# A graph network's encoder on one core: turning the normalized x of pairs 2 to 5 off the matrix engine

## The chip, the core and the metric

The kernel runs on one core of one Trainium2 chip. The core has five engines with a queue each: TensorE (PE in the rows; its weight loads are PEld), VectorE (DVE), ScalarE (ACT), GpSimd (POOL) and SyncE (SP, which here only issues DMAs; SPq is its queue). They work side by side and meet at semaphores. The metric is the device time of one run in microseconds (us); less is better.

## The reference

1250 nodes with 1024 features, 40,000 edges of two types. A relational graph convolution comes first, then a residual network with an encoder, three graph layers and a decoder. The part that this case is about is the encoder:

```python
x = _layernorm(x + L0(x))                         # x1 in the kernel
# L1:
h = layernorm(x, ln_in_g, ln_in_b)                # (x - m) * rsqrt(v + eps) * g + b
h = relu(h @ W1 + b1)                             # 1024 -> 512
h = h @ W2 + b2                                   # 512 -> 256
for i in range(3):
    z = h + segment_sum(h[src], dst)              # then two small products, a norm, a residual
    ...
delta = relu(h @ Wd1 + bd1) @ Wd2 + bd2
return layernorm(x + delta, out_g, out_b)
```

## The kernel before, in words

The 1250 nodes are T = 10 tiles of P = 125 rows. The encoder takes them in five pairs, called chunks here: chunk c holds tiles 2c and 2c+1. Features must lie on the partitions for the product with W1, so each normalized tile is turned from [125 nodes x 1024] to eight blocks [128 features x 125].

For chunk c the work runs through four engines:

- **GpSimd** (`second_norm`, L368) writes the normalized tile, without gain and bias, into one of two buffers `xh`.
- **TensorE** (`turn_chunk`, L823) turns both tiles by 16 products with the identity into four PSUM banks (0 to 3). These are the MATMULs of L830.
- **ScalarE and VectorE** take them out of PSUM, times gain plus bias, into `hT`: ScalarE four of the 16 blocks (`weigh_first`, L523), VectorE twelve (`weigh_turned`, L1318, instructions of L1325).
- **TensorE** (`chunk_of_3`, L834) then multiplies W1 with `hT` in four groups f = 0 to 3 of eight products (L845; the trace counts two records for each fp32 product, so 64 a chunk; a transpose is one record), which alternate between banks 4 and 5; ScalarE takes each group out with a relu (`relus_of_3`, L532, instructions of L537). Group f + 2 waits for the relu of group f, since it uses its bank. Group 1 of chunk 0 also waits for `res_done` of the last tile (the residual sum of L1283), which frees bank 5. Then the product with W2 (L855, 16 records a chunk) waits for all four relus, and VectorE adds the bias into `h` (`first_h`, L1328).

TensorE's order in chunk c is: the four groups of W1, the transposes of chunk c + 1, the product with W2. Chunks 0 to 3 run in a loop, chunk 4 behind it; four of the five chunks so hold transposes, and those of chunk 0 stand ahead of the encoder.

The order is written by hand on every engine. Beside chunk 0, VectorE and ScalarE still finish the norms of the last tiles (`into_encoder`, L1350ff.): they pass small results to and fro, and ScalarE's relus of groups 0 and 1 stand between these steps in its queue. SyncE issues, in this order: W1 in four parts with the last tile of x, W2 (L316), `wa_s` (L329), three rows of 1024 spread over 125 partitions (`bd2_b`, `go_b`, `bo_b`, L332), two of 768 (`bb_b`, `ng_b`, L325), and after the encoder the next weights.

Of the kernel before, what the change touches and what calls it, by code (L numbers as in the profile page):

```python
# [25 lines left out]
P = 125  # L26
T = N // P
# [30 lines left out]
def graph_kernel(nc, x, src, dst, typ, ln_w, w_rel, w_root, conv_b, wo, g_in, b_in, w1, b1, w2, b2,  # L58
                 wa, ba, wb, bb, ng, nb, wd1, bd1, wd2, bd2, g_out, b_out, out):
    with ExitStack() as ctx:  # L60
# [60 lines left out]
        def x1(t):  # L121
# [14 lines left out]
        assert end <= adj1_end, (end, adj1_end)  # L136

# [11 lines left out]
        assert end4 <= root_base, (end4, root_base)  # L149
        (w5, junk), end = stack(y_base + size([P, T, HB], F32) + size([128, K2, HB], F32) + size([128, K1, 2 * P], F32), [  # L150
# [80 lines left out]
        half_done, out_half = sem("half_done"), sem("out_half")  # L231
        out_done = [sem(f"out_done{u}") for u in range(2)]
# [24 lines left out]

        def zeros(n):

            return zero[:, 0:1].rearrange("p (a b) -> p a b", a=1).broadcast_to([P, T, n])  # L260

        @block.sync
        def _(sp):
# [65 lines left out]
            sp.dma_start(wa_s[:], wa[0].rearrange("(k p) f -> p k f", p=128)).then_inc(wab_in, 16)  # L329
            sp.wait_ge(wo_mm, 1 + 2 * T)  # L330
# [4 lines left out]

            sp.wait_ge(h_mm, 1 + T)
# [20 lines left out]
        def _(pool):  # L357
# [11 lines left out]
            def second_norm(t):  # L369
                pool.wait_ge(ln2_shift, t + 1)  # L370
                if t >= 2:
                    pool.wait_ge(xhT_ps, 2 * t - 2)
                pool.tensor_scalar(xh[:, t % 2], x1(t), small2[:, 2, t:t + 1], small2[:, 3, t:t + 1],  # L373
                                   ALU.mult, ALU.add).then_inc(xh_ready, 1)
# [11 lines left out]
            for t in range(4):  # L386
                second_norm(t)
            pool.wait_ge(fin_in, 48)
            pool.tensor_tensor(bo_b[:], bo_b[:], bd2_b[:], ALU.subtract).then_inc(bo_less, 1)
            for c in range(T // 2):  # L390
                for t in (2 * c + 4, 2 * c + 5):
# [20 lines left out]
        def _(act):  # L412
# [118 lines left out]

            def relus_of_3(c, blocks):  # L532
                for f in blocks:
                    if f == 0:
                        act.wait_ge(h_mm, 1 + c * 2)
                    act.wait_ge(r1_mm, 1 + c * K1 + f + 1)
                    act.activation(r1T[:, f], pb[:, 4 + f % 2, 0:2 * P],  # L537
                                   ACT.Relu, bias=b1_c[:, f:f + 1]).then_inc(r1_done, 1)
# [24 lines left out]
            relus_of_3(0, range(2, K1))  # L563
# [5 lines left out]
            for c in range(1, T // 2):  # L569
                weigh_first(c)  # L570
                for t in (2 * c - 2, 2 * c - 1):
                    high_part(t, t + 1)
                relus_of_3(c, range(K1))
# [125 lines left out]
        def _(pe):  # L699
# [124 lines left out]
            def turn_chunk(c):  # L824
                for u in range(2):
                    pe.wait_ge(xh_ready, c * 2 + u + 1)
                    for q in range(2):
                        for i in range(4):
                            k = 4 * q + i
                            ins = pe.transpose(pb[:, 2 * u + q, i * P:(i + 1) * P],  # L830
                                               xh[:, u, k * 128:(k + 1) * 128], ident[0:P, 0:P])
                        ins.then_inc(xhT_ps, 1)

            def chunk_of_3(c, last):  # L834
                pe.wait_ge(hT_lo, 1 + c + 1)
                pe.wait_ge(hT_hi, 1 + c + 1)
                pe.wait_ge(r1_done, 1 + c * K1)
                for f in range(K1):
# [5 lines left out]
                    for k in range(KD):  # L844
                        ins = pe.matmul(pb[:, 4 + f % 2, 0:2 * P], w1_s[:, k, f * 128:(f + 1) * 128], hT[:, k],  # L845
                                        start=(k == 0), stop=(k == KD - 1))
                    ins.then_inc(r1_mm, 1)
                if not last:
                    turn_chunk(c + 1)
# [50 lines left out]
            with pe.Fori(0, T // 2 - 1) as c:  # L900
                chunk_of_3(c, False)
# [160 lines left out]
        def _(dve):  # L1062
# [265 lines left out]

            def first_h(c):
# [19 lines left out]
            def into_encoder():  # L1349

                dve.wait_ge(consts_in, 16 * 5)
                weigh_turned(0)
                first_shift(T - 2)
# [9 lines left out]
                weigh_turned(1)  # L1363
# [149 lines left out]
```

## Time and profile before

| | |
|---|---|
| median of 3 runs | 591.04 us (590.6 to 591.4) |
| the profiled execution | 590.85 us, of which the span of its core is 589.0 us |
| granted TensorE clock, mean | 0.994 of full speed; full in every stretch of the encoder |
| busy shares of the span | TensorE 97%, VectorE 65%, ScalarE 38%, GpSimd 15% |
| the encoder in the span | from 276.2 us (first product with W1) to 369.3 us (first product of the graph layer) |

In the rows, times are us from the start of the span, unless marked ns. A row of a timeline gives the start, the length and the engine of a run of like instructions, its line, what it writes and reads, and how many there were; brackets at its end give the idle time ahead of it and what ended it. Matmul records overlap, so the start of the next row tells more than the end of one.

### The profile page before, as it was taken

How to read it: one execution, taken by the hardware profiler on the slowest of the kernel's cores; microseconds unless marked ns; L12 is line 12 of the kernel's file. 1: busy time of each engine (PE TensorE's matmuls, PEld its weight loads, DVE VectorE, ACT ScalarE, POOL GpSimd, SP SyncE). 2: the span in 40 equal slices, each digit the busy share in tenths (PEclk: the TensorE clock that was granted, in tenths of full speed). 3: DMA queues.
4: the chain of work that ended last, by engine and by line, in shares of the span. 5: the costliest groups of instructions: out<-in, count | busy, mean ns of one | idle time of the engine just before them, and what ended most of it. 6: DMA issues, size and time to landing. Idle time of an engine off the chain costs nothing.

```text
span 589.0 us, 8351 instructions
## 1 busy us (share of the span) xinstructions
PE 570.4 (97%) x2582; PEld 394.8 (67%) x2582; DVE 385.1 (65%) x996; ACT 223.1 (38%) x455; POOL 88.5 (15%) x70
## 2 busy tenths in 40 slices
PE   7999999999999999999999999999999999999992
PEld 3565655555567677675888888877877867455540
DVE  8599999888857888889503330018748667755464
ACT  5444344432213546553412221012223134266555
POOL 3000000000000000003065513401202230132230
PEclk9999999999999999999999999999999999999997
DMA  8510011111031112128300000600100100021123
GB/s 268 144 36 7 28 36 35 35 35 35 0 83 45 35 42 66 35 79 215 139 37 0 0 0 1 221 3 2 38 0 0 36 1 0 2 70 53 53 70 105
DMA packets 20897, 30.74 MB, mean 52 GB/s; under 512 B 5441, under 2 KB 15155, under 8 KB 20864
## 3 DMA queue, kind: packets, MB, share of 16 engines
q1 hardware_dynamic: 20710, 30.07, 17.1%
q8 instruction: 17, 0.28, 0.2%
q10 hardware_dynamic: 154, 0.26, 0.1%
q14 instruction: 16, 0.13, 0.1%
HBM read 25.20 MB, written 5.12 MB: 51 GB/s over the span
## 4 chain that ended last, share of the span: by engine, by line
PE 88%; DVE 3%; issue 2%; DVEq 2%; ACT 1%; SPq 1%; DMA 1%; POOL 0%
PE banks L726 15%; PE banks L925 12%; PE banks L1011 12%; PE banks L845 12%; PE banks L815 5%; PE banks L874 5%; PE banks L712 5%; PE banks L876 4%; PE banks L947 4%; PE banks L937 4%; PE banks L855 3%; PE banks L1001 3%; PE banks L819 2%; DVEq L1164 1%; PE banks L830 1%
## 5 line engine op out<-in xcount | busy, mean ns | idle before, releaser
L726 PE MATMUL banks<-w_all,xnT 128*125 128x429 f32 x320 | 129.3, 527 | 0.4 <-DMA w_all<-in_L_gnn_W_rel 0.4
L726 PEld LDWEIGHTS banks<-w_all,xnT 128*125 128x125 f32 x320 | 54.0, 188 | 30.1 <-issue 28.4
L1182 DVE TENSOR_TENSOR adj<-adj,banks 125x220 f32 x160 | 60.8, 380 | 17.3 <-PE banks L712 17.0
L845 PE MATMUL banks<-hT,w_s 128*128 128x250 f32 x320 | 68.7, 375 | 0.1
L845 PEld LDWEIGHTS banks<-hT,w_s 128*128 128x128 f32 x320 | 60.2, 189 | 8.8 <-issue 1.9
L874 PE MATMUL banks<-y_hi,adj 125*125 125x288 f32 x200 | 55.2, 304 | 0.9 <-DVE small L1241 0.9
L712 PEld LDWEIGHTS banks<-oh_code,oh_low 125*128 125x128 bf16 x320 | 30.5, 97 | 35.8 <-issue 30.5
L876 PE MATMUL banks<-y_lo,adj 125*125 125x286 f32 x200 | 53.6, 295 | 0.0
L1154 DVE TENSOR_TENSOR oh_code<-iota_c,edge 125x880 bf16<-125x880 f16 x82 | 50.0, 610 | 0.0
L1325 DVE TENSOR_SCALAR hT<-banks,g_c,b_c 128x125 f32<-128x125 f32 x60 | 19.4, 401 | 45.1 <-PE banks L830 45.0
L925 PE MATMUL banks<-adj,h_hi 125*128 125x250 f32 (+1 forms) x180 | 48.2, 367 | 0.0
L373 POOL TENSOR_SCALAR xh<-x_first,small 125x1024 f32<-125x1024 f32 x6 | 7.4, 1238 | 260.5 <-DVE adj L1269 260.4
L712 PE MATMUL banks<-oh_code,oh_low 125*128 125x220 bf16 x320 | 44.7, 260 | 1.9 <-DVE oh_code L1154 0.9
L925 PE MATMUL banks<-adj,h_lo 125*128 125x250 f32 (+1 forms) x180 | 45.6, 353 | 0.0
L1011 PE MATMUL banks<-wd_s,dT 128*125 128x512 f32 x96 | 42.7, 592 | 0.0
L874 PEld LDWEIGHTS banks<-y_hi,adj 125*125 125x125 f32 x200 | 37.1, 186 | 7.7 <-issue 6.1
L434 ACT ACTIVATE xnT<-banks,lnw 128x125 f32<-128x125 f32 x80 | 22.6, 377 | 50.1 <-PE banks L720 50.1
L378 POOL TENSOR_TENSOR h_lo<-h,h_hi 125x256 fp32r<-125x256 f32 x30 | 21.8, 732 | 108.0 <-ACT h_hi L567 108.0
L876 PEld LDWEIGHTS banks<-y_lo,adj 125*125 125x125 f32 x200 | 37.3, 186 | 0.0
L815 PE MATMUL banks<-wo_s,yT 128*125 128x512 f32 x80 | 36.0, 592 | 0.0
L1150 DVE TENSOR_TENSOR oh_low<-iota_l,edge 125x512 bf16<-125x512 f16 x82 | 34.3, 419 | 0.2 <-issue 0.2
L925 PEld LDWEIGHTS banks<-adj,h_hi 125*128 125x128 f32 x180 | 29.8, 189 | 5.5 <-issue 1.4
(190 smaller groups left out, 875.0 us busy)
## 6 DMA issues: line engine op xcount, KB each, us to landing
xt<-in_x SPq DMA_DIRECT2D x15, 448.0 KB
out_x<-ot SPq DMA_DIRECT2D x9, 448.0 KB
w_s<-in_L_gnn_W SPq DMA_DIRECT2D x5, 512.0 KB, 5.9
xn<-in_x SPq DMA_DIRECT2D x5, 448.0 KB
wd_s<-in_L_gnn_Wd SPq DMA_DIRECT2D x1, 2048.0 KB, 13.1
w_all<-in_L_gnn_W_rel SPq DMA_DIRECT2D x6, 286.0 KB, 6.0
wo_s<-in_L_gnn_wo_weight SPq DMA_DIRECT2D x1, 1024.0 KB, 6.6
w_all<-in_L_gnn_W_root SPq DMA_DIRECT2D x3, 286.0 KB, 5.6
```

The costliest lines, as they stand in the source:

```text
L712: ins = pe.matmul(pb[:, b, q * R * C:(q + 1) * R * C], oh_low[:, b, q, :, j], oh_code[:, b, q, :, j], start=(j == 0), stop=(j == JH - 1))
L726: ins = pe.matmul(pb[0:P, 2 + 2 * v + n, 0:FH], xnT[:, u], w_all[:, u, n * FH:(n + 1) * FH], start=(u == 0), stop=(u == KD - 1))
L815: pe.matmul(pb[0:P, 5 + q], yT[:, i], wo_s[:, i, q * 512:(q + 1) * 512], start=(i == 0), stop=False)
L845: ins = pe.matmul(pb[:, 4 + f % 2, 0:2 * P], w1_s[:, k, f * 128:(f + 1) * 128], hT[:, k], start=(k == 0), stop=(k == KD - 1))
L874: pe.matmul(pb[0:P, b + r, 0:F + 2], mine, y_hi[:, s, r * (F + 2):(r + 1) * (F + 2)].bitcast(kind), start=(s == 0), stop=False)
L876: ins = pe.matmul(pb[0:P, b + r, w0:w0 + F], mine, y_lo[:, s, r * F:(r + 1) * F].bitcast(kind), start=False, stop=(s == T - 1))
L925: ins = pe.matmul(pb[:, 3 * f + c, 0:n], part[:, s, f * 128:(f + 1) * 128], adj[:, 0, s, c0:c0 + n], start=(s == 0 and part is h_hi), stop ...
L937: ins = pe.matmul(pb[:, 3 * f + c, 0:n], wa_s[:, k, f * 128:(f + 1) * 128], zT[:, k, c0:c0 + n], start=(k == 0), stop=(k == K2 - 1))
L1011: ins = pe.matmul(pb[0:P, 2 + 2 * u + q], (dT, dT_odd)[c % 2][:, k, u * P:(u + 1) * P], wd2_s[:, k, q * 512:(q + 1) * 512], start=(k == 0) ...
L1150: return dve.tensor_tensor(oh_low[:, b], both(iota_l, LOW), spread_out(edge[:, 0], g, LOW), ALU.is_equal)
L1154: return dve.tensor_tensor(oh_code[:, b], both(iota_c, R * C), spread_out(code, g, R * C), ALU.is_equal)
L1182: dve.tensor_tensor(cols, cols, window(b, q), ALU.add).then_inc(done, 1)
```

## The change

The transposes of chunks 1 to 4 leave TensorE. For these chunks:

- **VectorE** turns each `xh` tile in blocks of 32 by 32 (`turn_blocks`, one instruction for a tile, 128 partitions x 1024) into `xb`. Three rows of x are loaded once into partitions 125 to 127 of both `xh` buffers, so that they hold numbers. `xb` holds both tiles of a chunk.
- **SyncE** moves the blocks between the groups of 32 partitions (`move`): 16 DMAs a chunk from SBUF to SBUF, each 32 partitions x 2 tiles x 1 KB (64 KB, in 64 runs of 1 KB). They raise one semaphore by 256 in all.
- **ScalarE** applies gain and bias in place (`weigh_moved`, eight instructions 128 x 128 for a tile), one tile behind the relu of group 2 and one behind that of group 3 of the chunk before.
- **TensorE** multiplies W1 with `moved_to(c)`, which has 2 x 128 columns a block where `hT` has 250. The loops over chunks are written out. Chunk 0 keeps its transposes, its `hT` and its 250 columns.
- Odd chunks use the buffer `hT_m`, even ones `hT_z`, which shares its place with chunk 0's `hT`. The move of chunk 2 or later waits until the W1 product of the chunk before is through.
- GpSimd's norms of tiles 4 and 5 stand ahead of its wait for the spread rows, and later ones move up a chunk.

```diff
@@ SyncE
+            for u in range(2):
+                sp.dma_start(xh[P:128, u], x_t[0][0:128 - P]).then_inc(pad_in, 16)
...
             sp.dma_start(wa_s[:], wa[0].rearrange("(k p) f -> p k f", p=128)).then_inc(wab_in, 16)
+            def move(c):
+
+                sp.wait_ge(xb_turned, 2 * c)
+                if c >= 2:
+                    sp.wait_ge(r1_mm, 1 + (c - 1) * K1)
+                for g in range(4):
+                    for q in range(4):
+                        sp.dma_start(moved_to(c)[g * 32:(g + 1) * 32, :, q],
+                                     xb[q * 32:(q + 1) * 32, :, g]).then_inc(xb_moved, 16)
+
+            move(1)
             sp.wait_ge(wo_mm, 1 + 2 * T)
             for a, d in ((bd2_b, bd2), (go_b, g_out), (bo_b, b_out)):
...
+            for c in range(2, T // 2):
+                move(c)
@@ GpSimd
-                if t >= 2:
+                if 2 <= t < 4:
                     pool.wait_ge(xhT_ps, 2 * t - 2)
+                if t >= 4:
+                    pool.wait_ge(xb_turned, t - 3)
...
-            for t in range(4):
+            for t in range(6):
                 second_norm(t)
             pool.wait_ge(fin_in, 48)
@@ ScalarE
+            def weigh_moved(t):
+
+                c, u = t // 2, t % 2
+                act.wait_ge(xb_moved, 256 * c)
+                for k in range(KD):
+                    part = moved_to(c)[:, u, :, k * 32:(k + 1) * 32]
+                    ins = act.activation(part, part, ACT.Identity, scale=g_c[:, k:k + 1], bias=b_c[:, k:k + 1])
+                ins.then_inc(hT_set, 1)
...
-            relus_of_3(0, range(2, K1))
+            relus_of_3(0, [2])
+            weigh_moved(2)
+            relus_of_3(0, [3])
+            weigh_moved(3)
@@ TensorE, chunk_of_3
-                pe.wait_ge(hT_lo, 1 + c + 1)
-                pe.wait_ge(hT_hi, 1 + c + 1)
+                if c == 0:
+                    pe.wait_ge(hT_lo, 1 + 1)
+                    pe.wait_ge(hT_hi, 1 + 1)
+                else:
+                    pe.wait_ge(hT_set, 2 * c)
...
+                            ins = pe.matmul(pb[:, 4 + f % 2, 0:256].rearrange("p (u q n) -> p u q n", u=2, q=4), w,
+                                            moved_to(c)[:, :, :, k * 32:(k + 1) * 32], start=(k == 0), stop=(k == KD - 1))
                     ins.then_inc(r1_mm, 1)
-                if not last:
-                    turn_chunk(c + 1)
                 pe.wait_ge(r1_done, 1 + c * K1 + K1)
@@ VectorE
+            def turn_blocks(t):
+
+                u = t % 2
+                dve.wait_ge(xh_ready, t + 1)
+                if t < 4:
+                    dve.wait_ge(pad_in, 32)
+                else:
+                    dve.wait_ge(xb_moved, 256 * (t // 2 - 1))
+                dve.transpose(xb[:, u].rearrange("p g (k e) -> p k g e", e=32),
+                              xh[:, u].rearrange("p (k g e) -> p k g e", g=4, e=32)).then_inc(xb_turned, 1)
...
-            with dve.Fori(1, T // 2 - 1) as c:
-                weigh_turned(c + 1)
+            for c in range(1, T // 2):
+                if c + 2 < T // 2:
+                    turn_blocks(2 * c + 4)
+                    turn_blocks(2 * c + 5)
                 first_h(c)
-            first_h(T // 2 - 1)
```

Where it moves instructions is best seen in the order itself. VectorE at the entry to the encoder, before (L1325 is the taking out of chunk 0, L1295 and L1297 are norm constants, L1283 is the residual of the last tile, for which group 1 of chunk 0 waits):

```order
L1289 BN_AGGR mv<-st_99 125x2
L1325 TENSOR_SCALAR hT<-banks,g_c,b_c 128x125 x12
L1295 RECIPROCAL small_98<-small_98 125x1
L1297 SCALAR_TENSOR_TENSOR small_98<-mv,small_98 125x1
L1283 SCALAR_TENSOR_TENSOR xt<-xt,banks 125x1024
L1286 BN_STATS st_99<-xt 125x6
```

The same place now (L1393 is the instruction of `turn_blocks`, L1339 the residual):

```order
L1345 BN_AGGR mv<-st_99 125x2
L1381 TENSOR_SCALAR hT<-banks,g_c,b_c 128x125 x12
L1393 STREAM_TRANSPOSE xb<-xh 128x8x4x32 x2
L1351 RECIPROCAL small_98<-small_98 125x1
L1353 SCALAR_TENSOR_TENSOR small_98<-mv,small_98 125x1
L1339 SCALAR_TENSOR_TENSOR xt<-xt,banks 125x1024
L1342 BN_STATS st_99<-xt 125x6
```

Two transposes of 1024 columns stand ahead of the last residual and of all that follows it. The twelve instructions of `hT` for each of chunks 1 to 4 are gone, and two transposes a chunk stand in other places.

ScalarE from the relu of group 1 of chunk 0 on, before (L537 are relus, L520 the last norm's root, L528 the taking out, L567 the split of h):

```order
L537 ACTIVATE r1T<-banks,b_c 128x250
L520 ACTIVATE small_98<-mv,epsc 125x1
L537 ACTIVATE r1T<-banks,b_c 128x250 x2
L528 ACTIVATE hT<-banks,b_c,g_c 128x125 x4
L567 CAST h_hi<-h 125x256 x2
L537 ACTIVATE r1T<-banks,b_c 128x250 x4
```

And now (L580 are relus, L572 the instructions of `weigh_moved`):

```order
L580 ACTIVATE r1T<-banks,b_c 128x250
L554 ACTIVATE small_98<-mv,epsc 125x1
L580 ACTIVATE r1T<-banks,b_c 128x250
L572 ACTIVATE hT_m<-hT_m,b_c,g_c 128x4x32 x8
L580 ACTIVATE r1T<-banks,b_c 128x250
L572 ACTIVATE hT_m<-hT_m,b_c,g_c 128x4x32 x8
L580 ACTIVATE r1T<-banks,b_c 128x250
L613 CAST h_hi<-h 125x256 x2
L580 ACTIVATE r1T<-banks,b_c 128x250 x2
L572 ACTIVATE hT_z<-hT_z,b_c,g_c 128x4x32 x8
```

Eight instructions stand between the relu of group 2 and that of group 3, and eight behind it.

SyncE around the first move, now; before, the 16 DMAs of L356 were not there and nothing else differed:

```order
L335 DMA w_s<-in_L_gnn_W 128x4x256
L348 DMA wa_s<-in_L_gnn_layer_Wa 128x2x256
L356 DMA hT_m<-xb 32x2x256 x16
L362 DMA bd_b<-in_L_gnn_bd 125x1024
L362 DMA go_b<-in_L_gnn_out_g 125x1024
L362 DMA bo_b<-in_L_gnn_out_b 125x1024
L344 DMA bb_b<-in_L_gnn_layer_bb 125x768
L344 DMA ng_b<-in_L_gnn_layer_ng 125x768
L356 DMA hT_z<-xb 32x2x256 x16
```

The first move stands between `wa_s` and the spread rows, the second behind them.

## Rows read from the trace of the kernel before

**Rows 1.** The page: busy time, share of the span and instructions of each engine.

```profile
PE 570.4 (97%) x2582; PEld 394.8 (67%) x2582; DVE 385.1 (65%) x996; ACT 223.1 (38%) x455; POOL 88.5 (15%) x70
```

**Rows 2.** Chain of waits, 300 to 440 us: start, length, what.

```profile
314.09 13.72 PE banks L845 x64
327.81 1.71 PE banks L830 x16
329.52 3.46 PE banks L855 x16
...
365.42 0.48 ACT r1T L537
...
365.94 3.72 PE banks L855 x16
```

**Rows 3.** Timeline of TensorE, chunk 0 and the last chunk.

```profile
276.17 13.76 PE L845 MATMUL banks<-hT,w_s 128*128 128x250 f32 x64
289.77 1.87 PE L830 MATMUL banks<-ident,xh 125*128 125x125 f32 x16
291.48 3.62 PE L855 MATMUL banks<-w_s,r1T 128*125 128x256 f32 x16
295.16 13.76 PE L845 MATMUL banks<-hT,w_s 128*128 128x250 f32 x64
...
351.70 13.69 PE L845 MATMUL banks<-hT,w_s 128*128 128x250 f32 x64
365.94 3.72 PE L855 MATMUL banks<-w_s,r1T 128*125 128x256 f32 x16 [0.56 <-ACT r1T L537]
```

**Rows 4.** Timeline of VectorE at the entry to the encoder.

```profile
271.94 3.88 DVE L1325 TENSOR_SCALAR hT<-banks,g_c,b_c 128x125 f32<-128x125 f32 x12
...
275.93 0.16 DVE L1297 SCALAR_TENSOR_TENSOR small<-mv,small 125x1 f32<-125x1 f32 x1
276.21 1.22 DVE L1283 SCALAR_TENSOR_TENSOR xt<-xt,banks 125x1024 f32<-125x1024 f32 x1
...
282.59 0.16 DVE L1295 RECIPROCAL small<-small 125x1 f32<-125x1 f32 x1 [1.24 <-ACT small L509]
```

**Rows 5.** Timeline of ScalarE beside chunk 0.

```profile
270.16 1.49 ACT L528 ACTIVATE hT<-banks,b_c,g_c 128x125 f32<-128x125 f32 x4
...
281.93 0.45 ACT L537 ACTIVATE r1T<-banks,b_c 128x250 f32<-128x250 f32 x1
...
285.75 0.45 ACT L537 ACTIVATE r1T<-banks,b_c 128x250 f32<-128x250 f32 x1
...
287.65 0.45 ACT L537 ACTIVATE r1T<-banks,b_c 128x250 f32<-128x250 f32 x1
```

**Rows 6.** Groups of ScalarE by shape, from 200 us on: SBUF to SBUF.

```profile
L567 ACT CAST h_hi<-h 125x256 fp32r<-125x256 f32 x30 | 12.2, 406 | 41.5 <-DVE h L1425 24.3 <-DVE h L1332 17.2
L514 ACT ACTIVATE x_rest<-x_rest,small 125x1024 f32<-125x1024 f32 x3 | 3.7, 1239 | 0.0
```

**Rows 7.** Stretches: busy time of each engine, clock, DMA share, GB/s.

```profile
276.00:282.00 6.00, 5.96 (x30) 5.27 (x29) 4.62 (x10) 1.41 (x3) 0.00 (x0) 1.00 0.94 265
...
286.00:290.00 4.00, 4.00 (x22) 3.51 (x21) 1.70 (x5) 0.88 (x4) 0.00 (x0) 1.00 0.32 129
...
298.00:302.00 4.00, 4.00 (x20) 3.59 (x19) 0.00 (x0) 0.47 (x1) 4.00 (x4) 1.00 0.08 26
```

**Rows 8.** Timeline of SyncE's queue: start and length of an issue.

```profile
279.01 0.71 SPq L325 DMA_DIRECT2D bb_b<-in_L_gnn_layer_bb  x1
...
369.69 0.39 SPq L319 DMA_DIRECT2D wb_s<-in_L_gnn_layer_Wb  x1
```

**Rows 9.** DMA issues of the whole span: count, KB each, median us to landing.

```profile
bd_b<-in_L_gnn_bd SPq DMA_DIRECT2D x1, 500.0 KB
...
bb_b<-in_L_gnn_layer_bb SPq DMA_DIRECT2D x1, 375.0 KB
...
ba_c<-in_L_gnn_layer_ba SPq DMA_DIRECT2D x3, 1.0 KB, 2.8
```

More of the change, by code:

```diff
@@ L136, in graph_kernel @@
         assert end <= adj1_end, (end, adj1_end)
+        (xb,), end = stack(z_base, [("xb", [128, 2, 4, 32 * KD], F32)])
+        assert end <= adj1_end
         adj_x = at(top[0], "adj_x", [P, R, T, ND], F32)
@@ L149, in graph_kernel @@
         assert end4 <= root_base, (end4, root_base)
+        z_zt = end4 - sum(size(a, F32) for a in ([P, 5, HB], [P, 2, 6], [P, 8], [P, 2, 2], [P, 2, 4], [P, 2, 4], [P, 2, 4]))
+        (hT,), end = stack(z_zt, [("hT", [128, KD, 2 * P], F32)])
+        (hT_z,), end = stack(z_zt, [("hT_z", [128, 2, 4, 32 * KD], F32)])
+        assert end <= root_base
         (w5, junk), end = stack(y_base + size([P, T, HB], F32) + size([128, K2, HB], F32) + size([128, K1, 2 * P], F32), [
@@ L231, in graph_kernel, with moved_to @@
         half_done, out_half = sem("half_done"), sem("out_half")
+        pad_in, xb_turned, xb_moved, hT_set = sem("pad_in"), sem("xb_turned"), sem("xb_moved"), sem("hT_set")
+        def moved_to(c):
+            return hT_m if c % 2 else hT_z
         out_done = [sem(f"out_done{u}") for u in range(2)]
@@ L256, in load_w, with r1_of @@
                               w_rel[r, part].rearrange("(k p) f -> p k f", p=128)).then_inc(w_in[q], 16)
+        def r1_of(c, f):
+            n = 128 if c else P
+            return pb[:, 4 + f % 2, 0:2 * n].rearrange("p (u n) -> p u n", u=2)[:, :, 0:P]
         def zeros(n):
@@ L390, in _ @@
             for c in range(T // 2):
-                for t in (2 * c + 4, 2 * c + 5):
+                for t in (2 * c + 6, 2 * c + 7):
                     if t < T:
@@ L536, in relus_of_3 @@
                     act.wait_ge(r1_mm, 1 + c * K1 + f + 1)
-                    act.activation(r1T[:, f], pb[:, 4 + f % 2, 0:2 * P],
+                    act.activation(r1T[:, f].rearrange("p (u n) -> p u n", u=2), r1_of(c, f),
                                    ACT.Relu, bias=b1_c[:, f:f + 1]).then_inc(r1_done, 1)
@@ L569, in _ @@
             for c in range(1, T // 2):
-                weigh_first(c)
+                relus_of_3(c, [0])
                 for t in (2 * c - 2, 2 * c - 1):
                     high_part(t, t + 1)
-                relus_of_3(c, range(K1))
+                relus_of_3(c, [1, 2])
+                if c + 1 < T // 2:
+                    weigh_moved(2 * c + 2)
+                relus_of_3(c, [3])
+                if c + 1 < T // 2:
+                    weigh_moved(2 * c + 3)
             for t in (T - 2, T - 1):
@@ L844, in chunk_of_3 @@
                     for k in range(KD):
-                        ins = pe.matmul(pb[:, 4 + f % 2, 0:2 * P], w1_s[:, k, f * 128:(f + 1) * 128], hT[:, k],
-                                        start=(k == 0), stop=(k == KD - 1))
+                        w = w1_s[:, k, f * 128:(f + 1) * 128]
+                        if c == 0:
+                            ins = pe.matmul(pb[:, 4 + f % 2, 0:2 * P], w, hT[:, k], start=(k == 0), stop=(k == KD - 1))
+                        else:
+                            ins = pe.matmul(pb[:, 4 + f % 2, 0:256].rearrange("p (u q n) -> p u q n", u=2, q=4), w,
+                                            moved_to(c)[:, :, :, k * 32:(k + 1) * 32], start=(k == 0), stop=(k == KD - 1))
                     ins.then_inc(r1_mm, 1)
-                if not last:
-                    turn_chunk(c + 1)
                 pe.wait_ge(r1_done, 1 + c * K1 + K1)
@@ L898, in _ @@
             project(T - 1)
-            with pe.Fori(0, T // 2 - 1) as c:
+            for c in range(T // 2 - 1):
                 chunk_of_3(c, False)
@@ L1352, in into_encoder @@
                 weigh_turned(0)
+                turn_blocks(2)
+                turn_blocks(3)
                 first_shift(T - 2)
@@ L1362, in into_encoder @@
                 dve.wait_ge(adj_self, T)
-                weigh_turned(1)
+                turn_blocks(4)
+                turn_blocks(5)
                 first_h(0)
```

11 lines of the change are left out of this document (6 added, 5 removed).

## The prediction

> **What bounds the kernel now.** The page's busy shares come first: TensorE is busy for 97% of the span [rows 1]. The chain of waits over the encoder says the same of this stage: it stays on TensorE through the chunks, and the transposes of L830 are a piece of it, 1.71 us in each of four chunks [rows 2]. So work taken off TensorE there can shorten the time. The next view is TensorE's timeline, which gives the period of a chunk: from 295.16 to 351.70 three chunks pass, 18.85 us each [rows 3]. The last chunk has no transposes, and it shows what they cover: behind group 3 TensorE is idle for 0.56 us until the relu is through [rows 2, 3]. The timelines of VectorE and ScalarE beside chunk 0 come last, for there the change puts new work into queues that TensorE waits for. The reader should see how near they run: group f of chunk 0 is due at 276.17 plus 3.40 f (279.57, 282.97, 286.37; a quarter of 13.60, the distance from 276.17 to 289.77 [rows 3]). The relus that groups 2 and 3 wait for end at 282.38 and 286.20 [rows 5], and the residual for group 1 at 277.43 [rows 4]. The spare time is 0.6, 0.2 and 2.1 us.
>
> **What chunks 1 to 3 gain.** Gone are 1.71 us of transposes. Exposed instead is the wait for the last relu. The last chunk is the model: from its first product with W1 to its first with W2 are 365.94 - 351.70 = 14.24 us, and W2 takes 3.46 [rows 2, 3]. That is 17.70 us. The columns go from 250 to 256. By columns the 13.72 us would grow by 0.33; by the pace of L855, whose records have 256 columns (3.46 / 16 = 0.216 us against 13.72 / 64 = 0.214 [rows 2]), by 0.12. I take 0.2. The period is 17.9 us, 0.95 less than before, and three of them give 2.85 us. The last chunk only pays the 0.2. The loops that are written out I cost at nothing, since TensorE shows no idle time at a chunk's seam [rows 3].
>
> The Trainium skill, in "VectorE: DVE Perf Modes", section "The three transpose paths", lists 390 ns on TensorE for a block of 128 by 128 and 311 ns on VectorE, bf16. By that VectorE would be the cheaper place. This trace has 107 ns for one of TensorE's 16 transposes, 1.71 / 16 [rows 2], and no transpose by VectorE at all, so it bears out no such advantage; the sum goes by the nearest rows, next.
>
> **What chunk 0 pays on VectorE.** Two transposes of 1024 columns stand ahead of the last residual. The nearest row is another VectorE instruction of 1024 columns, 1.22 us [rows 4]; with the gap to the next, 1.25 each, 2.5 in all. The bounds: 512 columns' worth each, 0.6 (1.2 in all), were it to go at twice that pace; and 0.316 us for each of the eight blocks of 128, the pace of the twelve instructions of L1325 (3.88 us [rows 4]), 2.5 each, 5.0 in all. The value is the nearest row's. VectorE was free at 276.09 and the residual began at 276.21 [rows 4], so 0.1 is absorbed and everything behind shifts by 2.4. It does shift: from there VectorE and ScalarE hand each other the norms of the last tiles (a wait of 1.24 us of VectorE for ScalarE stands among them [rows 4]), and the relus of groups 0 and 1 stand in ScalarE's queue between these steps [rows 5]. Then:
> - group 1 waits for the residual, which ends at 279.8: due 279.57, stall 0.3;
> - group 2 waits for the relu that now ends at 284.8: due 283.3, stall 1.5; it ends at 288.2;
> - group 3 waits for the relu that now ends at 288.6: stall 0.4; it ends at 292.0.
>
> **What chunk 0 pays on ScalarE.** The relu of group 2 starts at 287.65 + 2.4 = 290.05 and ends at 290.5. Then come eight instructions 128 x 128, SBUF to SBUF. The four of L528 take 1.49 us; if one is as long as a relu, 0.45, they follow each other at (1.49 - 0.45) / 3 = 0.35 us [rows 5]. The two SBUF shapes, 406 ns for 256 columns and 1239 for 1024, give 1.085 ns a column and 0.27 us for 128 [rows 6]. So 2.1 to 2.8; I take 2.75, near the row of the same operation. The relu of group 3 runs from 293.2 to 293.7, and W2 begins at 293.75 instead of 291.48, 1.7 us after group 3 has ended. The next chunk begins 3.5 later, at 297.25: 2.1 us later than the 295.16 of before. The transposes of chunk 1, 1.71 us, are already taken off in that. The second eight end by 296.5, ahead of chunk 1.
>
> **The moves.** The last VectorE transpose ends at 278.25. An issue takes 0.39 us on a quiet queue and 0.71 on a busy one [rows 8], with 0.04 between. W2 and wa_s are still under way until about 282 [rows 7]. At 0.42, 16 issues end at 285.0; at 0.75, at 290.2. Landing comes 2.8 us after the issue, by the smallest transfer [rows 9], from about 287.4 to 292.6. Needed is 290.5: with the faster pace nothing is paid. No row shows a copy from SBUF to SBUF.
>
> Behind the first move stand the spread rows, 3 x 500 + 2 x 375 KB = 2.30 MB [rows 9]. They run at 129 GB/s with a DMA share of 0.32, 5 of 16 engines [rows 7]: 17.9 us, and by the windows they ended at about 298.8 (26 GB/s over 298 to 302). Now they begin at about 285.5 and end at 303.4. The second move is issued from 293.2 on (VectorE turns tiles 4 and 5 after its last norm, at 290.6 to 293.1), behind them in the same queue. On the five engines its 64 runs of 1 KB each take 62 ns at the rate of 265 GB/s over 16 engines [rows 7], 4.0 us, so it lands at about 307.4 plus a tail of 1, 308.4. ScalarE can take it at 308.1 (297.25, three groups of 3.45, a relu), and group 3 ends at 311.05, so 2.75 us of work is hidden if it begins by 308.3. Between 0 (all of it early) and 3 us (busy issue pace, below) I take 0.3. The moves of chunks 3 and 4 have some 5 us to spare even though the last waits for chunk 2's product, and VectorE's waits for them stand ahead only of the bias of h, which is wanted a chunk later.
>
> The Trainium skill, "DMA: Bandwidth & Descriptors", section "Why a DMA increments its semaphore by 16 and not by 1", says that a DMA is split over the largest number up to 16 that divides its outer sizes: 125 partitions use 5 engines, 32 use 16. The trace agrees for the spread rows (0.32 of 16). The Trainium skill has further, on the same page under "Queues, rings and completion order", that each engine takes its ring in order, by which the second move can't pass them; no run shown here tests that.
>
> **The sum.** +2.1 (start of chunk 1), -2.85 (periods of chunks 1 to 3), +0.2 (last chunk), +0.3 (second move): -0.25 us. What follows the encoder starts from the same state as before. The profiled execution took 590.85 us, which gives 590.6; it lies 0.19 below the median of the runs, which gives 590.8, my forecast.
>
> **The rivals.**
> - *The full saving comes through* (faster). ScalarE's eight take 2.1 instead of 2.75, the second move is in time, VectorE's transpose goes a little faster (1.1), W1's pace is 0.12 dearer instead of 0.2. The terms: 2.1 - 0.65 - 0.3 = 1.15; -3.1; 0.12; 0. Sum -1.85, 589.2. For it: each term has a row on that side. Against: all must fall so. Chance 0.28, over 589.0 to 589.8.
> - *The second move decides* (slower). One place, ScalarE's wait ahead of the relu of group 3 of chunk 1; it costs from a landing after 308.3 on, one for one, and TensorE stands still. At the busy pace of 0.75 us the first move ends its issue at 290.2 and lands at 292.6, 2.1 late in chunk 0; chunk 1 starts at 299.35 and its limit is 310.4. The spread rows end at 290.6 + 17.9 = 308.5, the move lands at 313.5, 3.1 late. Sum -0.55 + 2.1 + 3.1 = +4.65, 595.7 at the full price; with only half of that delay some 593. For it: 0.71 us for an issue beside full traffic, and an unseen kind of copy. Against: the queue is quiet from 282 on. Chance 0.18.
> - *VectorE's transpose is twice as dear*, 2.5 us each (slower): 2.4 more through chunk 0, while the second move then is in time: -0.55 + 2.5 = +1.95, 593.0. The Trainium skill's 311 ns a block ("VectorE: DVE Perf Modes", "The three transpose paths"), eight of them, would be 2.5 us, an estimate from that page; it is for one block an instruction and need not hold for eight in one. For this rival speaks the pace of L1325, against it the 1.22 us of one instruction of 1024 columns [rows 4]. Chance 0.12.
> - *The change doesn't do what it says*: the order shows that the transposes are gone. No chance is left for it.
>
> The forecast has 0.42. About 0.2%, 1.2 us, is what a measurement of this kernel can tell from no change. Faster: most of the first rival and a little of the forecast's spread, 0.28. Slower: the second and third, 0.29. The same: 0.43. The range from 588.9 to 593.3 leaves out the full price of the second rival.
>
> **What would show it.** The line that L830 has become should have 16 records (chunk 0's) and take 1.7 us; TensorE idle times of about 0.3, 1.5, 0.4 and 1.7 us in chunk 0, the last three ended by ScalarE, and 0.56 us in each later chunk; a VectorE transpose of 1.2 us; ScalarE's instructions of `weigh_moved` 0.35 apart; periods of 17.9 us. The forecast is wrong if the issues of a move take over 0.6 us each, if ScalarE waits for a DMA ahead of `weigh_moved(2)` or `(4)`, if W1 with 256 columns in runs of 32 takes over 14.1 us, or if the stages behind the encoder move.

## The result, and the profile after

The changed kernel takes 603.53 us (median of 5 runs, 602.96 to 604.4), the kernel before 591.04 us (five runs too). The ratio is 1.0215, with a 95% interval of 1.0204 to 1.0226: slower by 12.5 us. The forecast was 590.8 us, with 588.9 to 593.3 as its range. It was wrong in size and in kind. The second rival, that the second move decides, is what happened, at more than twice the price that I gave it, and not by its path: it had the first move land late, at 292.6, and that one landed at 290.7. The profiled execution took 604.39 us, with a span of 602.1 us against 589.0.

The timeline of TensorE after the change, which answers to [rows 3], shows where the 13.1 us between the two spans lie (L901 and L903 are W1, with 250 and 256 columns; L911 is W2):

```profile
276.11 7.11 PE L901 MATMUL banks<-hT,w_s 128*128 128x250 f32 x32
284.51 3.65 PE L901 MATMUL banks<-hT,w_s 128*128 128x250 f32 x16 [1.29 <-ACT r1T L580]
288.34 3.65 PE L901 MATMUL banks<-hT,w_s 128*128 128x250 f32 x16 [0.18 <-ACT r1T L580]
294.35 3.72 PE L911 MATMUL banks<-w_s,r1T 128*125 128x256 f32 x16 [2.36 <-ACT r1T L580]
297.91 13.98 PE L903 MATMUL banks<-hT_m,w_s 128*128 128x256 f32 x64
322.31 6.16 PE L911 MATMUL banks<-w_s,r1T 128*125 128x256 f32 x16 [10.42 <-ACT r1T L580]
328.31 13.98 PE L903 MATMUL banks<-hT_z,w_s 128*128 128x256 f32 x64
342.84 3.72 PE L911 MATMUL banks<-w_s,r1T 128*125 128x256 f32 x16 [0.56 <-ACT r1T L580]
346.40 13.98 PE L903 MATMUL banks<-hT_m,w_s 128*128 128x256 f32 x64
...
364.49 13.98 PE L903 MATMUL banks<-hT_z,w_s 128*128 128x256 f32 x64
...
382.39 0.92 PE L981 MATMUL banks<-adj,h_hi 125*128 125x250 f32 x3
```

From the start of chunk 0 to that of chunk 1 are 21.80 us instead of 18.99 [rows 3]: +2.8. Chunk 1 takes 30.40 instead of 18.85: +11.55. Chunks 2 and 3 take 18.09 each: -0.76 each. The last, up to the first product of the graph layer, takes 17.90 instead of 17.6: +0.3. Together that is 13.1, the difference of the spans. The gain that the change is made for is there, in the two chunks that nothing disturbs. One chunk loses nearly eight times what these two gain.

TensorE's idle time of 10.42 us in chunk 1 is put down to ScalarE's relu. The relu was not slow; the chain of waits of the changed kernel tells what stood ahead of it:

```profile
294.26 5.26 SPq L356
...
310.56 0.60 SPq L356
...
311.20 7.49 DMA hT_z<-xb
...
318.72 3.18 ACT hT_z L572 x8
321.90 0.36 ACT r1T L580
322.31 6.16 PE banks L911 x16
```

The first issue of the second move holds SyncE's queue for 5.26 us, the last one begins at 310.56, and its data lands 7.49 us after 311.20. Only then do ScalarE's eight instructions run, and only behind them the relu. SyncE's queue, which answers to [rows 8]:

```profile
278.16 11.17 SPq L356 DMA_DIRECT2D hT_m<-xb  x16
289.38 0.49 SPq L362 DMA_DIRECT2D bd_b<-in_L_gnn_bd  x1
...
291.10 3.06 SPq L344 DMA_DIRECT2D ng_b<-in_L_gnn_layer_ng  x1
294.26 17.54 SPq L356 DMA_DIRECT2D hT_z<-xb  x16
321.18 10.74 SPq L356 DMA_DIRECT2D hT_m<-xb  x16
342.36 10.18 SPq L356 DMA_DIRECT2D hT_z<-xb  x16
```

Sixteen issues of a move take 10.2 us with nothing in their way and 17.5 behind the spread rows. The stretches of the changed kernel, which answer to [rows 7] (columns as there), show the traffic and the clock:

```profile
298.00:300.00 2.00, 2.00 (x11) 1.77 (x10) 0.43 (x2) 0.00 (x0) 0.00 (x0) 1.00 0.32 131
...
312.00:316.00 4.00, 0.00 (x0) 0.00 (x0) 0.00 (x0) 0.00 (x0) 4.00 (x3) 1.00 0.38 91
316.00:320.00 4.00, 0.00 (x0) 0.00 (x0) 1.22 (x2) 1.28 (x4) 0.95 (x1) 0.63 0.03 9
320.00:324.00 4.00, 1.69 (x4) 1.41 (x5) 1.16 (x2) 4.00 (x11) 2.37 (x2) 0.50 0.19 47
324.00:328.00 4.00, 4.00 (x12) 3.16 (x12) 0.42 (x1) 1.33 (x4) 0.00 (x0) 0.59 0.41 101
```

At 298 the spread rows run at a share of 0.32 and 131 GB/s, as before, but they were issued 13 us later (from 289.38 instead of 276.28). And the granted clock, full all through the encoder before, falls while TensorE stands still for 10.42 us (0.63 on average from 316 to 320) and is 0.50 from 320 to 324, 1.2 GHz instead of 2.4. W2 of chunk 1 takes 6.16 us instead of 3.72, so 2.4 us of the loss are the clock.

### The profile page after: what moved, and what is told of

Its sections match the earlier page's. It is cut to its first block, busy times and chain, and to the rows that moved or that the text cites. A ratio compares the mean times of both kernels' runs of the same rounds, so it can differ in the third digit from the quotient of the medians.

```text
span 602.1 us, 8227 instructions
## 1 busy us (share of the span) xinstructions
PE 568.8 (94%) x2518; PEld 390.0 (65%) x2518; DVE 379.2 (63%) x956; ACT 240.8 (40%) x503; POOL 88.5 (15%) x70
## 4 chain that ended last, share of the span: by engine, by line
PE 78%; SPq 6%; DVE 5%; DMA 3%; ACT 3%; issue 2%; DVEq 2%
PE banks L777 14%; PE banks L981 12%; PE banks L1067 11%; PE banks L903 6%; PE banks L866 5%; PE banks L763 4%; SPq L356 4%; PE banks L1003 4%; PE banks L993 4%; PE banks L930 4%; PE banks L932 4%; PE banks L911 3%; PE banks L1057 3%; PE banks L870 2%; DVEq L1220 1%
## 5 line engine op out<-in xcount | busy, mean ns | idle before, releaser
L1399 DVE TENSOR_TENSOR h<-banks,b_b 125x256 f32<-125x256 f32 x10 | 4.2, 425 | 56.3 <-PE banks L911 56.3
L911 PE MATMUL banks<-w_s,r1T 128*125 128x256 f32 x80 | 21.0, 422 | 14.5 <-ACT r1T L580 14.5
L981 PEld LDWEIGHTS banks<-adj,h_lo 125*128 125x128 f32 x180 | 30.1, 189 | 4.6
```

The costliest lines, as they stand in the source:

```text
L911: ins = pe.matmul(pb[0:P, 6 + u, 0:HB], r1T[:, k, u * P:(u + 1) * P], w2_s[:, k], start=(k == 0), stop=(k == K1 - 1))
L981: ins = pe.matmul(pb[:, 3 * f + c, 0:n], part[:, s, f * 128:(f + 1) * 128], adj[:, 0, s, c0:c0 + n], start=(s == 0 and part is h_hi), stop ...
```

## The experiments

All ratios are to the kernel before, timed beside them.

**What holds the second move.** In `e1_parts` the spread rows are loaded in two DMAs each:

```diff
-                sp.dma_start(a[:], spread(d)).then_inc(fin_in, 16)
+                for rows in row_parts:                     # 112 and 13 partitions
+                    sp.dma_start(a[rows], spread(d)[rows]).then_inc(fin_in, 16)
```

(and so for `bb_b`, `ng_b`, `nb_b`, with the waits for them doubled).

> The changed kernel, with each of the five spread rows loaded in two DMAs, 112 and 13 partitions, instead of one of 125. Theory A (the spread rows, on 5 of 16 DMA engines, hold the second move back in the same rings): on 16 engines their 2.3 MB are through in about 8 us, the second move lands by 307, and TensorE's idle time of 10.42 us ahead of W2 of chunk 1 shrinks to about 0.56, with no fall of the granted clock. Time 603.5 - 9.9 - 2.4 (W2 at full clock) = about 591.2 us. Theory B (a move is slow by itself: 0.64 us an issue and a slow copy from SBUF to SBUF): the idle time stays above 8 us and the time within 1.5 us of 603.5.

Measured: 593.33 us (592.48 to 593.95), ratio 1.0038 [1.0025, 1.0051]; 10.2 us less than the changed kernel, 2.1 more than theory A had. TensorE's timeline of `e1_parts`, and SyncE's queue:

```profile
294.65 3.72 PE L914 MATMUL banks<-w_s,r1T 128*125 128x256 f32 x16 [2.40 <-ACT r1T L583]
298.21 13.98 PE L906 MATMUL banks<-hT_m,w_s 128*128 128x256 f32 x64
312.74 3.72 PE L914 MATMUL banks<-w_s,r1T 128*125 128x256 f32 x16 [0.56 <-ACT r1T L583]
```

```profile
294.87 10.20 SPq L358 DMA_DIRECT2D hT_z<-xb  x16
```

The idle time of 10.42 us is 0.56, W2 has its full clock, and the second move's issues take 10.20 us, not 17.54. Nothing of the moves themselves was changed. So the spread rows, which kept 5 of the 16 engines busy, held it. In `e1_parts` the DMA share is 0.90 from 292 to 296, at 267 GB/s, and the last of the three rows of 1024 is in after 9.8 us (289.7 to 299.5) instead of 16.9.

The run tells something else: with the stall gone, the change is still slower than the kernel before, by 1.2 us of span. Chunk 0 is 2.9 us longer, three periods of 18.09 give back 2.3, the last chunk costs 0.3; the rest of the 1.2 stands outside these. The median lies 0.85 above the profiled execution, which was the fastest run and had the highest mean clock (0.995; the slowest, 593.95, had 0.991). The kernel before with the same edit, `b2_parts`, is the control:

> The kernel before, with only the five spread rows in 112 and 13 partitions. Nothing waits for them in the kernel before, so no change: within 0.3 us of it. If it is faster, e1_parts and all built on it owe that part to something else than the moves.

Measured: 591.06 us (590.67 to 591.76), ratio 1.0002 [0.9993, 1.0011]: no change.

**Rings or engines.** `e2_act_rows` takes the five rows from SyncE and has ScalarE issue them, ahead of its `second_sd(T - 3)`:

```diff
+            act.wait_ge(rel0_added, T)
+            act.wait_ge(wo_mm, 1 + 2 * T)
+            for a, d in ((bd2_b, bd2), (go_b, g_out), (bo_b, b_out)):
+                act.dma_start(a[:], spread(d)).then_inc(fin_in, 16)
...
```

> The changed kernel, with the five spread rows issued by ScalarE's queue at about 276 us, where ScalarE idles, instead of by SyncE behind the first move. They still use 5 engines, but rings of their own, and start 13 us earlier. Theory A: the second move is in time (idle ahead of W2 of chunk 1 about 0.56 us); the first move now shares the five engines with the rows and lands 2 to 4 us later than at 290.7, which TensorE waits for in chunk 0. Time 593 to 595 us. Theory B: both moves as slow as before, 603 us. If ScalarE's five issues take more than 5 us in all, chunk 0 gets longer by what is over.

Measured: 606.02 us (605.04 to 606.27), ratio 1.0246 [1.0231, 1.0262]. Both of my theories missed. The second move is in time (0.56 us in chunk 1), but it was issued from 305.36 on, when the rows were through, so this does not speak for theory A. And the first move is far later than I expected. ScalarE and TensorE of `e2_act_rows`:

```profile
302.86 3.19 ACT L567 ACTIVATE hT_m<-hT_m,b_c,g_c 128x128 f32<-128x128 f32 x8 [12.58 <-DMA hT_m<-xb]
```

```profile
306.46 5.43 PE L913 MATMUL banks<-w_s,r1T 128*125 128x256 f32 x16 [14.37 <-ACT r1T L575]
```

It lands at 302.8 instead of 290.7, with the rows under way at 120 to 133 GB/s from 292 until about 304, at a share of 0.31 to 0.34, five of 16 engines. A queue of its own for the rows does not free the move. Nor does it help to put the rows behind the second move, `e3_rows_later` (GpSimd's wait for them moves too, behind its low parts of chunk 0):

```diff
+            move(2)
             for a, d in ((bd2_b, bd2), (go_b, g_out), (bo_b, b_out)):
...
-            for c in range(2, T // 2):
+            for c in range(3, T // 2):
                 move(c)
```

> The changed kernel, with the five spread rows issued behind the second move instead of ahead of it, and GpSimd's wait for them behind its low parts of chunk 0. Theory A: the second move lands at about 306 and chunk 1 has no stall but 0.56 us; the third move now stands behind the rows and lands late, at 327 to 333, so that chunk 2 stalls by up to 6 us. Time 592 to 599 us. Theory B: chunk 1 still stalls for 8 us or more, 602 us or more.

Measured: 598.03 us (595.75 to 599.39), ratio 1.0108 [1.0085, 1.0131]. Chunk 1 has its 0.56 us, and the stall stands in chunk 2, 3.35 us, as theory A says. ScalarE and TensorE of `e3_rows_later`:

```profile
331.64 3.19 ACT L573 ACTIVATE hT_m<-hT_m,b_c,g_c 128x128 f32<-128x128 f32 x8 [2.70 <-DMA hT_m<-xb]
```

```profile
335.23 5.41 PE L912 MATMUL banks<-w_s,r1T 128*125 128x256 f32 x16 [3.35 <-ACT r1T L581]
```

The third move's issues were not held up here (10.60 us for 16), and yet it landed 7.2 us after the last of them. So a move behind the rows is late also where its issuer is free. Part of the scatter is probably the clock: in the profiled run it fell with the 2.46 us stall in chunk 0 and again in chunk 2 (W2 took 5.21 and 5.41 us instead of 3.72). In the changed kernel's and in `e1_parts`' profiled run a stall of about the same length left the clock at full. So a stall of 2.4 us in chunk 0 costs W2 1.5 us in some runs and nothing in others.

**What an issue costs.** `e5_split` cuts each DMA of a move in two, on top of `e1_parts`:

```diff
-                        sp.dma_start(moved_to(c)[g * 32:(g + 1) * 32, :, q],
-                                     xb[q * 32:(q + 1) * 32, :, g]).then_inc(xb_moved, 16)
+                        for u in range(2):
+                            sp.dma_start(moved_to(c)[g * 32:(g + 1) * 32, u, q],
+                                         xb[q * 32:(q + 1) * 32, u, g]).then_inc(xb_moved, 16)
```

> Built on e1_parts. Each DMA of a move is cut in two, one a tile: 32 DMAs of 32 KB (32 runs of 1 KB) in place of 16 of 64 KB. If the 0.60 us of an issue are a fixed price of a DMA from SBUF to SBUF, a move's issues take 20 us and chunks stall: 600 us or more. If they go by the runs, an issue takes about 0.3 us and nothing changes: 593. A copy whose pace goes by bytes on the engines would leave the issues at 0.4 and the landing where it is.

Measured in a single run: 624.7 us. TensorE stalls in each of chunks 0 to 3, by 12.48, 5.45, 5.38 and 4.12 us. The queue of `e5_split`:

```profile
278.26 21.45 SPq L359 DMA_DIRECT2D hT_m<-xb  x32
```

An issue of 32 runs takes 0.59 us in the median, one of 64 runs 0.60. So for these two sizes it is a fixed price of a DMA from SBUF to SBUF, where a load from HBM took 0.39 [rows 8].

**What chunk 0 pays.** `b1_turns` is the kernel before, with two transposes by VectorE and nothing else:

```diff
                 weigh_turned(0)
+                for t in (2, 3):
+                    dve.wait_ge(xh_ready, t + 1)
+                    dve.transpose(xb[0:96, t % 2]..., xh[0:96, t % 2]...)
                 first_shift(T - 2)
```

> The kernel before, with nothing changed but two transposes by VectorE (tiles 2 and 3, 96 partitions x 1024, result unused) ahead of the last residual. Theory A: they take 1.2 us each and shift the chain of the last norms by 2.1 us; TensorE stalls for 1.3 us ahead of group 2 and 0.2 us ahead of group 3 of chunk 0, as in the changed kernel: +1.5 us, 592.5. Rival: they are hidden, and the stalls come from something else of the change: 591.0.

Measured: 592.94 us (592.74 to 593.45), ratio 1.0028 [1.0016, 1.004], so +1.6 us, as theory A says. Its TensorE timeline has the same two stalls as the changed kernel (its chunk 0 as a whole is 2.0 us longer: 21.00 instead of 18.99):

```profile
284.72 3.65 PE L847 MATMUL banks<-hT,w_s 128*128 128x250 f32 x16 [1.29 <-ACT r1T L539]
288.55 3.65 PE L847 MATMUL banks<-hT,w_s 128*128 128x250 f32 x16 [0.18 <-ACT r1T L539]
```

The rest of chunk 0's loss is ScalarE's. `s1_share`, on top of `e1_parts`, gives one tile of each pair to VectorE and puts ScalarE's behind the relu of group 3:

```diff
-            relus_of_3(0, [2])
-            weigh_moved(2)
-            relus_of_3(0, [3])
+            relus_of_3(0, [2, 3])
             weigh_moved(3)
@@ VectorE
+                for k in range(KD):
+                    part = moved_to(c)[:, 0, :, k * 32:(k + 1) * 32]
+                    ins = dve.tensor_scalar(part, part, g_c[:, k:k + 1], b_c[:, k:k + 1], ALU.mult, ALU.add)
```

> Built on e1_parts. VectorE applies gain and bias to the first tile of each moved pair, ScalarE only to the second, behind the relu of group 3. Theory: in e1_parts ScalarE's eight instructions (3.19 us) ahead of the relu of group 3 of chunk 0, released by the first move at 290.7, cost 2.40 - 0.56 = 1.84 us of TensorE's time, and the same stall lowers the granted clock in part of the runs. Both go: idle of 0.56 us ahead of W2 of chunk 0, all later periods 18.09 as they were, 593.3 - 1.8 - 0.6 = about 591 us. Rival: the first move lands too late for chunk 1 in any case, and the stall only moves to the head of chunk 1: above 592.5.

Measured: 589.93 us (589.67 to 590.28), ratio 0.9983 [0.9974, 0.9992]. W2 of chunk 0 waits for 0.56 us. This is the first of the series that beats the kernel before, by 1.0 us, about 1 us better than its theory had.

**Covering the last relu.** `s2_ahead` has TensorE do group 0 of the next chunk ahead of W2, from chunk 1 on (`groups_of_3` and `second_of_3` are the two halves of `chunk_of_3`):

```diff
+            for c in range(1, T // 2):
+                groups_of_3(c, range(1, K1))
+                if c + 1 < T // 2:
+                    groups_of_3(c + 1, [0])
+                second_of_3(c)
```

> Built on s1_share. From chunk 1 on, TensorE does group 0 of the next chunk ahead of W2, so that this covers the last relu; VectorE weighs ten of the 16 blocks of a pair and ScalarE six, ahead of the relu of group 3. Theory: the 0.56 us exposed in chunks 1 to 3 go, 1.7 us in all: about 589.5 us, periods of 17.5 us. Rival: the gain is used up by waits for the blocks (moves land too late for group 0, which starts 3.5 us earlier): 591 or more.

Measured: 590.03 us (589.44 to 592.4), ratio 0.9988 [0.9978, 0.9998]. The time lies between what theory and rival had, no better than `s1_share`; the mechanism is the rival's. Periods of later chunks are 17.26 us (355.82 less 338.56), but group 0 of chunk 2 waits for its blocks, 2.39 us, and the clock is lower in some runs (a mean of 0.990 and 0.991 in the three slowest, at least 0.993 in the others).

`s3_shift` also has ScalarE take 12 of the 16 blocks of chunk 0 out of PSUM and VectorE only four, so that VectorE's transposes begin at 273.3 instead of 275.9:

```diff
+                act.wait_ge(xhT_ps, c * 4 + 4)
+                for k in range(KD):
+                    ins = act.activation(hT[:, k, P:2 * P], pb[:, 2 + k // 4, ...], ACT.Identity, ...)
@@ VectorE, weigh_turned
-                for u, q in ((0, 1), (1, 0), (1, 1)):
+                for u, q in ((0, 1),):
```

> Built on s2_ahead. In chunk 0 ScalarE, idle there until 282, takes 12 of the 16 transposed blocks out of PSUM and VectorE four, so that VectorE's two transposes begin 2.5 us earlier. Theory: the stalls of TensorE ahead of groups 2 and 3 of chunk 0 (1.29 and 0.18 us) come from those transposes shifting the chain of the last norms by 2.1 us; they shrink to 0.3 or less, the first move begins 2 us earlier, and the time falls by 1.2 us against s2_ahead, to about 588.3. Rival: the stalls stay, since ScalarE's part of the chain is what is late: no change.

Measured: 589.42 us (587.47 to 592.82), ratio 0.9984 [0.9968, 1.0]. The theory had 588.3. Chunk 0's stall of 1.29 us is gone, as it says, but the one in chunk 2 grew to 2.92 and the times scatter over 5 us, the slow ones again at the lower mean clock (0.989 to 0.992). To see the shift by itself, `s5_share_shift` puts it on `s1_share`, without group 0 ahead:

> s1_share with ScalarE's larger part in chunk 0 from s3_shift, and TensorE's order left as it was. Theory: s1_share has no late move, so the one stall that is left (1.29 us ahead of group 2 of chunk 0) goes: 589.9 - 1.2 = 588.7 us, and all runs near each other, since nothing lowers the clock. Rival: the scatter of s3_shift (587.5 to 592.8) comes from the shift itself: it scatters here too.

Measured: 588.72 us (588.28 to 588.84), ratio 0.996 [0.9947, 0.9974]: as expected, and steady.

**The late blocks of chunk 2.** `s4_issue` is `s3_shift` with four of a move's 16 DMAs issued by ScalarE's queue, and nine blocks of 16 for VectorE instead of ten:

```diff
+            def move_rest(c):
+                act.wait_ge(xb_turned, 2 * c)
+                act.wait_ge(r1_mm, 1 + (c - 1) * K1)
+                for q in range(4):
+                    act.dma_start(moved_to(c)[96:128, :, q], xb[q * 32:(q + 1) * 32, :, 3]).then_inc(xb_moved, 16)
```

> s3_shift with four of the 16 DMAs of moves 2 to 4 issued by ScalarE's queue at the head of a chunk, where ScalarE idles, and 9 blocks by VectorE, 7 by ScalarE. Theory: an issue costs 0.64 us of the issuing queue, so the second move lands 2.5 us earlier, and the wait of 2.9 us ahead of group 0 of chunk 2, with the fall of the clock behind it, goes: 587 us, without runs above 589. Rival: DMAs of two queues share the engines and land no earlier: as s3_shift.

Measured: 588.94 us (588.32 to 589.47), ratio 0.9963 [0.9949, 0.9976]. The theory had 587. The blocks land at 306.0, 1.6 us earlier and not 2.5, and the wait is still 1.99 us. VectorE of `s4_issue`, chunk 1's blocks and chunk 2's, and two instructions of the latter by themselves:

```profile
290.81 2.40 DVE L1422 TENSOR_SCALAR hT_m<-hT_m,g_c,b_c 128x128 f32<-128x128 f32 x9 [1.27 <-DMA hT_m<-xb]
...
305.96 5.26 DVE L1422 TENSOR_SCALAR hT_z<-hT_z,g_c,b_c 128x128 f32<-128x128 f32 x9 [9.82 <-DMA hT_z<-xb]
```

```profile
305.96 1.15 DVE L1422 TENSOR_SCALAR hT_z<-hT_z,g_c,b_c 128x128 f32<-128x128 f32 x1 [9.82 <-DMA hT_z<-xb]
307.03 2.39 DVE L1422 TENSOR_SCALAR hT_z<-hT_z,g_c,b_c 128x128 f32<-128x128 f32 x1
```

and GpSimd's:

```profile
304.67 4.67 POOL L420 TENSOR_TENSOR x_first<-x_first,bd_b 125x1024 f32<-125x1024 f32 x2
```

The first of nine instructions takes 1.15 us and the second 2.39 instead of 0.34. They end, within 0.1 us, when GpSimd's first and second one end (its two take 2.36 each, from 304.67 and 306.98 on), and with the other seven at their usual pace that is the whole 5.26. `s6_apart` keeps the two engines apart:

```diff
+                if c + 2 < T // 2:
+                    pool.wait_ge(hT_vec, c + 2)
                 for t in (2 * c, 2 * c + 1):
                     with_bd2(t)
```

> s4_issue with one wait more: GpSimd adds the row bd2 to a pair of tiles only after VectorE has applied gain and bias to its blocks of the next pair but one. Theory: in s4_issue VectorE's nine instructions took 5.26 us ahead of chunk 2 and 2.40 us ahead of chunk 1, because one of them waited for a GpSimd instruction that was running; kept apart they take 2.4 us, group 0 of chunk 2 starts without the idle time of 1.99 us, and the time falls by 2 us to about 587.0. Rival: the slowness comes from the spread rows' or the moves' DMA traffic, and stays: 588.9.

Measured: 586.53 us (586.42 to 588.52), ratio 0.9933 [0.992, 0.9947], 4.5 us less than the kernel before. VectorE and TensorE of `s6_apart`:

```profile
305.76 2.40 DVE L1424 TENSOR_SCALAR hT_z<-hT_z,g_c,b_c 128x128 f32<-128x128 f32 x9 [10.09 <-DMA hT_z<-xb]
```

```profile
295.03 13.98 PE L919 MATMUL banks<-hT_m,w_s 128*128 128x256 f32 x64
308.84 3.68 PE L919 MATMUL banks<-hT_z,w_s 128*128 128x256 f32 x16
312.36 3.62 PE L929 MATMUL banks<-w_s,r1T 128*125 128x256 f32 x16
315.81 10.52 PE L919 MATMUL banks<-hT_z,w_s 128*128 128x256 f32 x48
```

The blocks land when they did in `s4_issue` (305.8), so DMA traffic, the rival, was not what slowed VectorE. TensorE waits for nothing between 295.03 and the last chunk's relu.

## Why the prediction was wrong, point by point

- **Periods of chunks 2 and 3: right in kind, a gain of 0.76 us a chunk where I had 0.95.** 18.09 us, forecast 17.9. The wait for the last relu is 0.56 us as in the last chunk of before. W1 with 256 columns in runs of 32 costs 0.29 us a chunk (342.84 - 328.31 = 14.53, before 14.24), where I took 0.2 of 0.12 to 0.33. The other 0.1 is W2: I took its 3.46 from the chain, but from its first product to the next chunk's first are 3.57 in the kernel before (332.93 - 329.36) and 3.56 now.
- **VectorE's price in chunk 0: right.** A transpose takes 1.22 us, as the nearest row said. The stalls ahead of groups 2 and 3 are 1.29 and 0.18, forecast 1.5 and 0.4, the 0.3 ahead of group 1 did not come, and `b1_turns` shows them to be the transposes' alone. The rival that VectorE's transpose is twice as dear is out.
- **ScalarE's price in chunk 0: right in kind, too small.** Idle 2.36 us ahead of W2, forecast 1.7. The eight instructions are 0.39 us apart (3.19 us for eight, one of them 0.48), not 0.35, and the first move landed at 290.7, 0.6 later than they could begin. Chunk 1 began at 297.91, forecast 297.25.
- **The step that failed: "The moves", the landing of the second one.** I had it at 308.4 against a limit of 308.3, and gave 0.3 us. It landed at 318.7, 10.3 later. Three terms were mis-sized. The issue: 0.60 us with 0.04 between, not the 0.42 that I took from a load on a quiet queue, so that the spread rows began at 289.4 instead of 285.5 (3.9 us). The passage of the rows: I reckoned 17.9 us from their bytes and a rate of 129 GB/s. The third one landed at 306.3, and the last two, 750 KB, need 6.0 at that rate (an estimate), so they were through at about 312.3, after 22.9 us (5.0 more). And the move behind them landed 6.4 us later, where I had 4 and a tail of 1 (1.4 more). `e1_parts` shows that the rows on five engines make the whole of the stall.
- **What the rows of before had said.** In the kernel before the five rows were issued from 276.28 on, and GpSimd could use the third at 293.90, 17.6 us later:

```profile
276.28 0.38 SPq L332 DMA_DIRECT2D bd_b<-in_L_gnn_bd  x1
```

```profile
293.90 2.36 POOL L389 TENSOR_TENSOR bo_b<-bo_b,bd_b 125x1024 f32<-125x1024 f32 x1 [20.89 <-DMA bo_b<-in_L_gnn_out_b]
```

By my own reading of [rows 7] they ended at about 298.8. That is 22.5 us from the first issue, and not the 17.9 of the rate, though part of that time was shared with W2 and `wa_s`. From 289.4 it gives 311.9, and a landing near 317.
- **What I left out: the clock.** I priced a late landing one for one. Behind 10.42 us of standing still TensorE runs at 1.2 GHz for W2, 2.4 us more. The two together are the +11.55 us of chunk 1 with the gain of that chunk taken off: 9.86 + 2.44 - 0.76 = 11.54.
- **The sum without the failed step.** From chunk 0 +2.8, three periods -2.3, the last chunk +0.3: about +0.8 us, where I had -0.55. So even a second move in time would have made the kernel no faster, and `e1_parts` bears that out.
- **The signs.** Of those that I named, one came: ScalarE waits for a DMA ahead of `weigh_moved(2)` (0.57 us) and of `weigh_moved(4)` (9.78 us). An issue of a move, at 0.60 us, stands at the bound that I gave.
- **The chances.** The second rival had 0.18 and 595.7 as its full price. An estimate that ends 0.1 us past its limit, for a transfer of a kind that the trace does not show, is as likely late as not. The rival deserved more than 0.18, and the range should have reached at least to its full price; even that lies 7.8 us below what was measured.
- **Slips in the sums**, which change nothing: by its own terms the second rival's first move lands at 292.3, not 292.6 (278.25 + 15 x 0.75 + 2.8), and the first rival adds up to -1.83.

The Trainium skill, "DMA: Bandwidth & Descriptors", section "Queues, rings and completion order", says that an engine goes round its queues packet by packet. `e2_act_rows` agrees in so far as the rows, in a queue of their own, still share engines with the move, which landed 12 us later. In what turns the engines served the two queues, no run here shows.

What stays open: why the first three spread rows take longer than their bytes at 129 GB/s, 11.9 us for 1.54 MB. It was 16.9 us in the changed kernel, 16.2 in `e3_rows_later` (303.9 to 320.1) and 17.6 in the kernel before. From 290 to 298 the changed kernel has a share of 0.32 to 0.35, as at full rate, but only 102 to 104 GB/s. Open too is what SyncE's slowed issues, 17.5 us instead of 10.2, added to the last 1.4 us; `e1_parts` removes both at once and does not part them. A variant with fewer DMAs a move, each over 128 partitions, wasn't tried. Nor do the runs tell why a stall of 2.4 us lowers the clock in some runs only.

## What to carry to other kernels

Work taken off the busiest engine is paid for in the queues that take it over: ask of each new wait what else uses the same DMA engines, and when they are through, by the landing in a trace and not by bytes and a rate. In this case a load spread over 125 partitions kept five of the 16 engines busy for long and made a move behind it late; the same load as 112 and 13 partitions let it through (593.3 us instead of 603.5). And a step that is timed to land within a microsecond of its limit should be moved, or given an even chance of being late.

## What the runs showed of the hardware that I had not expected

- A DMA from SBUF to SBUF held the issuing queue for 0.60 us with 64 runs of 1 KB and for 0.59 with 32 (medians of `e1_parts` and `e5_split`), with 0.04 between two; the five spread rows, loads from HBM behind the first move, took 0.34 to 0.49 where nothing held them up.
- A VectorE instruction from SBUF to SBUF with one tensor input (128 x 128, float32) waited for a running GpSimd instruction to end: 2.39 us instead of 0.34 (`s4_issue`). Kept apart, none took over 0.35 (`s6_apart`). The Trainium skill, "SBUF — State Buffer", section "Who interferes with whom", tells of a port pair that VectorE and GpSimd share and that one holds for a whole instruction; these rows agree with it. Not every instruction waits: two of VectorE's transposes took 2.36 us together from 308.07 on in `s6_apart`, as ever, beside GpSimd's instructions of the same kind (308.23 to 312.91). In the kernel before VectorE took these blocks from PSUM, 0.40 us each in all 60 instructions.
- TensorE's clock fell from 2.4 to 1.2 GHz in each of the three stalls of over 10 us (10.42, 14.37 and, in `e5_split`, 12.48; W2 took 6.16, 5.43 and 5.80 us instead of 3.72). In all three it was down while TensorE still stood idle. It fell too with `e5_split`'s stalls of 4.12, 5.38 and 5.45 us. With stalls of about 2.4 us it fell in some runs only: `e3_rows_later`'s W2 took 5.21 us behind a stall of 2.46, the changed kernel's 3.72 behind one of 2.36.
